# Attention outputs of two four-head units gathered in one PSUM bank, post-processed once per eight heads

## The reference

```python
x = x + 0.5 * ffn(layernorm(x), weight, bias, delta_w, delta_act)
x = x + attn(layernorm(x), wq, bq, wk, bk, wv, bv)
x = x + 0.5 * ffn(layernorm(x), weight, bias, delta_w, delta_act)

# attn: q, k, v = projections; rotary embedding on q and k; per head of 8 features:
scores = einsum('bhqd,bhkd->bhqk', q, k) / sqrt(8)
out = einsum('bhqk,bhkd->bhqd', softmax(scores), v)
```

## Time and profile before

| | us |
|---|---|
| runs | 550.89, 562.03, 566.96 |
| median | 562.03 |
| profiled execution | 559.28 |
| its span from first to last instruction | 557.5 |
| mean granted TensorE clock in it, share of full speed | 0.938 |

### The profile page before, as it was taken

One profiled execution on the slowest core, in us unless ns is written; L12 is line 12 of the kernel. 1 busy time (PEld: TensorE's weight loads), 2 busy tenths in 40 slices (PEclk: granted clock), 3 DMA queues, 4 the chain that ended last, 5 costly groups with the idle time before them and its releaser, 6 DMA issues.

```text
span 557.5 us, 10137 instructions
## 1 busy us (share of the span) xinstructions
PE 473.2 (85%) x2628; PEld 165.2 (30%) x2628; DVE 438.8 (79%) x1020; ACT 389.1 (70%) x754; POOL 229.7 (41%) x350
## 2 busy tenths in 40 slices
PE   2141889999999989999899889999999999998851
PEld 1121232333233333433233223333233323322211
DVE  6646999887998797978897688978897789888025
ACT  5556149787878776688768676878768787777840
POOL 8100156326662555437552564436553534112310
PEclk9985599999999997999899998999899999999995
DMA  6013411221122212221123112221222022200000
GB/s 170 7 47 89 127 51 48 88 86 50 49 87 86 69 50 63 71 88 30 55 84 106 41 48 86 76 68 30 71 79 89 31 76 87 76 3 2 20 1 19
DMA packets 27967, 34.89 MB, mean 63 GB/s; under 512 B 6278, under 2 KB 21260, under 8 KB 27916
## 3 DMA queue, kind: packets, MB, share of 16 engines
q1 hardware_dynamic: 26284, 33.94, 20.1%
q10 hardware_dynamic: 1632, 0.39, 0.3%
HBM read 21.34 MB, written 8.39 MB: 53 GB/s over the span
## 4 chain that ended last, share of the span: by engine, by line
PE 60%; DVE 18%; issue 8%; ACT 7%; POOL 5%; DVEq 1%; DMA 0%; POOLq 0%; ACTq 0%; SPq 0%
PE ot L1120 19%; PE sc L1107 16%; PE st L1096 13%; DVE negmax L893 8%; PE misc L1085 3%; PE misc L1043 3%; ACT probs L645 2%; PE misc L1060 2%; ACT feat_k L535 2%; DVE stats_f L761 1%; DVE amax_f L785 1%; PE misc L1068 1%; PE misc L1038 1%; PE misc L1077 1%; PE misc L1051 1%
## 5 line engine op out<-in xcount | busy, mean ns | idle before, releaser
L893 DVE TENSOR_REDUCE negmax<-sc 128x1 f32<-128x512 f32 x512 | 331.5, 683 | 60.8 <-PE sc L1107 60.0
L645 ACT ACTIVATE probs<-st 128x512 f32<-128x512 f32 x512 | 272.3, 602 | 78.4 <-PE st L1096 75.4
L1107 PE MATMUL sc<-feat_k,feat_q 96*128 96x512 bf16 x512 | 189.4, 398 | 11.8 <-DVE negmax L893 11.1
L1096 PE MATMUL st<-feat_q,feat_k 99*128 99x512 bf16 x512 | 160.3, 386 | 7.8 <-ACT probs L645 6.8
L1120 PE MATMUL ot<-probs,vfeat 128*32 128x512 f32 x1024 | 139.5, 618 | 1.0 <-ACT probs L645 1.0
L1107 PEld LDWEIGHTS sc<-feat_k,feat_q 96*128 96x128 bf16 x512 | 50.1, 98 | 167.8 <-DVE negmax L893 126.2
L1096 PEld LDWEIGHTS st<-feat_q,feat_k 99*128 99x128 bf16 x512 | 49.9, 99 | 80.7 <-ACT probs L645 51.9
L452 POOL TENSOR_SCALAR maxparts<-negmax 128x16 bf16<-128x16 f32 x32 | 8.3, 258 | 70.3 <-DVE negmax L893 70.3
L1027 PE MATMUL misc<-identb,xq_f 128*128 128x128 bf16 x64 | 6.8, 235 | 34.9 <-DVE xq_f L837 34.8
L494 POOL TENSOR_TENSOR xres<-xres,onorm 128x128 f32 (+1 forms) x31 | 14.1, 454 | 53.3 <-DVE onorm L910 53.3
L636 ACT COPY outT<-ot 128x512 f32<-128x512 f32 x32 | 18.8, 586 | 18.7 <-PE ot L1120 18.7
(11 more groups left out here) (134 smaller groups left out, 488.1 us busy)
## 6 DMA issues: line engine op xcount, KB each, us to landing
feat_q<-parts_q SPq DMA_DIRECT2D x96, 96.0 KB
feat_k<-parts_k SPq DMA_DIRECT2D x96, 96.0 KB
qkswap<-qkpre SPq DMA_DIRECT2D x32, 128.0 KB, 2.0
parts_q<-qkparts_q SPq DMA_DIRECT2D x24, 128.0 KB, 2.4
parts_k<-qkparts_k SPq DMA_DIRECT2D x24, 128.0 KB, 2.3
xres<-in_L_attn_x_dram SPq DMA_DIRECT2D x8, 256.0 KB, 4.6
out_dram<-xres SPq DMA_DIRECT2D x8, 256.0 KB, 2.4
feat_q<-maxrows ACTq DMA_DIRECT2D x32, 12.0 KB
```

Source lines behind the costliest of these rows:

```text
L645: nc.scalar.activation(probs[:, s % US, j * S:(j + 1) * S], st[:, bank(2 * s + j), :], ACT.Exp, scale=SCALE).then_inc(exp_done, 1)
L893: nc.vector.tensor_reduce(negmax[:, g, j:j + 1], sc[:, bank(16 * g + j), :], AX.X, ALU.max, negate=True).then_inc(sc_maxed, 1)
L1096: nc.tensor.matmul(st[:, bank(2 * s + j), :], feat["k"][par][0:MROWS, h, kb * P:(kb + 1) * P], feat["q"][par][0:MROWS, h, :], start=True, ...
L1107: nc.tensor.matmul(sc[:, bank(16 * g + j), :], feat["q"][par][0:SROWS, h, t * P:(t + 1) * P], feat["k"][par][0:SROWS, h, :], start=True, s ...
```

## The change

`times_v` of an odd unit now adds to the same bank as that of the even unit before it. For that the values of the heads of odd units are put 16 columns further to the right in their 32 (`values`), with the column of ones beside them; the columns of the other unit of the pair are zero, so each of the eight `times_v` of a pair adds zeros to the rows of the other unit. Only the first call of a pair starts the accumulation. `pairs` keeps only the turns of odd units: copy, transposes, reciprocal, normalisation and residual addition run once per pair, with the shapes of one unit for copy and transposes, 32 instead of 16 elements per row for the reciprocal, two products instead of one for the normalisation, and one addition of 256 elements per row in place of two of 128. The value copy becomes two of half the size, and the fills two more. The post-processings at slots 12 and 28 are gone, those at slots 4 and 20 stay.

```diff
@@ -122,4 +122,4 @@
         outT = sb("outT", [P, S])
-        recip = sb("recip", [P, T, UH])
-        onorm = sb("onorm", [P, T, UH, HD])
+        recip = sb("recip", [P, T, UH, 2])
+        onorm = sb("onorm", [P, T, 2, UH, HD])
         negmax = sb("negmax", [P, G, UH * T])
@@ -241,2 +241,15 @@
 
+        def values(par, u):
+
+            v = vfeat[par].rearrange("p t (g u i) v -> p (t g) u i v", u=2, i=UH)
+            return v[:, :, u, :, VW // 2 * u:VW // 2 * u + HD + 1]
+
+        def pair_of(b, g):
+
+            return 2 * b + g // 2
+
+        def pairs(u):
+
+            return [turn for turn in u if turn[2] % 2 == 1]
+
         def gate(eng):
@@ -378,3 +391,4 @@
                 fill(vfeat[i][:, :, :, :], 0.0)
-                fill(vfeat[i][:, :, :, HD:HD + 1], 1.0)
+                for u in range(2):
+                    fill(values(i, u)[:, :, :, HD:HD + 1], 1.0)
             assert done[0] == FILLS
@@ -489,7 +503,6 @@
 
-                u = G * b + g
-                pool.wait_ge(o_normed, u + 1)
-                n = UH * HD
-                cols = xb(b).rearrange("p (t d) -> p t d", t=T)[:, :, n * g:n * (g + 1)]
-                nc.gpsimd.tensor_tensor(cols, cols, onorm[:, :, :, :].rearrange("p t h d -> p t (h d)"),
+                n = 2 * UH * HD
+                pool.wait_ge(o_normed, pair_of(b, g) + 1)
+                cols = xb(b).rearrange("p (t d) -> p t d", t=T)[:, :, n * (g // 2):n * (g // 2 + 1)]
+                nc.gpsimd.tensor_tensor(cols, cols, onorm[:, :, :, :, :].rearrange("p t u i d -> p t (u i d)"),
                                         ALU.add).then_inc(x_attended, 1)
@@ -500,3 +513,3 @@
                         split_max(nb, g)
-                    for nb, _, g in turns_of_unit(b, par, s, OUT["add"], -1):
+                    for nb, _, g in pairs(turns_of_unit(b, par, s, OUT["add"], -1)):
                         if not hurried("f2", nb) or g < G - 1:
@@ -602,4 +615,5 @@
                     act.wait_ge(pv_done, 16 * (b - 1))
-                nc.scalar.copy(vfeat[par][:, :, :, 0:HD], misc[:, :].rearrange("p (t h d) -> p t h d", t=T, d=HD)
-                               ).then_inc(v_ready, 1)
+                v = misc[:, :].rearrange("p (t u i d) -> p t u i d", u=2, i=UH, d=HD)
+                for u in range(2):
+                    nc.scalar.copy(values(par, u)[:, :, :, 0:HD], v[:, :, u, :, :]).then_inc(v_ready, 1)
 
@@ -633,4 +647,4 @@
                 act.wait_ge(pv_done, 4 * u + 4)
-                if after(u):
-                    act.wait_ge(ot_turned, u)
+                if after(pair_of(b, g)):
+                    act.wait_ge(ot_turned, pair_of(b, g))
                 nc.scalar.copy(outT[:, :], ot[:, :]).then_inc(ot_out, 1)
@@ -656,3 +670,3 @@
                         load_max_rows(nb, npar, g)
-                    for nb, _, g in turns_of_unit(b, par, s, OUT["copy"], -1):
+                    for nb, _, g in pairs(turns_of_unit(b, par, s, OUT["copy"], -1)):
                         copy_out(nb, g)
@@ -755,3 +769,3 @@
                 else:
-                    dve.wait_ge(x_attended, G * b + G)
+                    dve.wait_ge(x_attended, 2 * b + 2)
                 if after(2 * b):
@@ -897,6 +911,5 @@
 
-                u = G * b + g
-                o = misc[:, :].rearrange("p (t h v) -> p t h v", t=T, v=VW)
-                dve.wait_ge(ot_turned, u + 1)
-                nc.vector.reciprocal(recip[:, :, :], o[:, :, :, HD]).then_inc(ot_recip, 1)
+                o = misc[:, :].rearrange("p (t i u v) -> p t i u v", t=T, i=UH, u=2)
+                dve.wait_ge(ot_turned, pair_of(b, g) + 1)
+                nc.vector.reciprocal(recip[:, :, :, :], o[:, :, :, :, HD]).then_inc(ot_recip, 1)
 
@@ -904,10 +917,10 @@
 
-                u = G * b + g
-                o = misc[:, :].rearrange("p (t h v) -> p t h v", t=T, v=VW)
-                dve.wait_ge(ot_recip, u + 1)
-                if after(u):
-                    dve.wait_ge(x_attended, u)
-                nc.vector.tensor_tensor(onorm[:, :, :, :], o[:, :, :, 0:HD],
-                                        recip[:, :, :].unsqueeze(3).broadcast_to([P, T, UH, HD]), ALU.mult
-                                        ).then_inc(o_normed, 1)
+                o = misc[:, :].rearrange("p (t i u v) -> p t i u v", t=T, i=UH, u=2)
+                dve.wait_ge(ot_recip, pair_of(b, g) + 1)
+                if after(pair_of(b, g)):
+                    dve.wait_ge(x_attended, pair_of(b, g))
+                for u in range(2):
+                    ins = nc.vector.tensor_tensor(onorm[:, :, u, :, :], o[:, :, :, u, 0:HD],
+                                                  recip[:, :, :, u].unsqueeze(3).broadcast_to([P, T, UH, HD]), ALU.mult)
+                ins.then_inc(o_normed, 1)
 
@@ -915,7 +928,6 @@
 
-                u = G * b + g
-                dve.wait_ge(o_normed, u + 1)
-                n = UH * HD
-                cols = xb(b).rearrange("p (t d) -> p t d", t=T)[:, :, n * g:n * (g + 1)]
-                nc.vector.tensor_tensor(cols, cols, onorm[:, :, :, :].rearrange("p t h d -> p t (h d)"),
+                n = 2 * UH * HD
+                dve.wait_ge(o_normed, pair_of(b, g) + 1)
+                cols = xb(b).rearrange("p (t d) -> p t d", t=T)[:, :, n * (g // 2):n * (g // 2 + 1)]
+                nc.vector.tensor_tensor(cols, cols, onorm[:, :, :, :, :].rearrange("p t u i d -> p t (u i d)"),
                                         ALU.add).then_inc(x_attended, 1)
@@ -925,3 +937,3 @@
                     mb, _, mg, ms = ahead(b, par, s)
-                    for nb, _, g in turns_of_unit(b, par, s, OUT["turn"] + 1, -1):
+                    for nb, _, g in pairs(turns_of_unit(b, par, s, OUT["turn"] + 1, -1)):
                         invert_sums(nb, g)
@@ -1063,3 +1075,3 @@
 
-                misc_free((v_ready, b + 1))
+                misc_free((v_ready, 2 * b + 2))
                 nc.tensor.matmul(misc[:, :], ones3[:, :], bias3[:, 0:D].unsqueeze(1).broadcast_to([PARTS, T, D]),
@@ -1080,5 +1092,4 @@
             def turn_out(b, g):
-                u = G * b + g
-                pe.wait_ge(ot_out, u + 1)
-                misc_free((o_normed, u + 1))
+                pe.wait_ge(ot_out, pair_of(b, g) + 1)
+                misc_free((o_normed, pair_of(b, g) + 1))
                 for t in range(T):
@@ -1113,6 +1124,6 @@
                 if kb == 0:
-                    if after(u):
-                        pe.wait_ge(ot_out, u)
+                    if g % 2 == 0 and after(pair_of(b, g)):
+                        pe.wait_ge(ot_out, pair_of(b, g))
                     if g == 0:
-                        pe.wait_ge(v_ready, b + 1)
+                        pe.wait_ge(v_ready, 2 * b + 2)
                 pe.wait_ge(exp_done, 2 * (US * u + UH * (kb // 2 + 1)))
@@ -1121,3 +1132,3 @@
                                            probs[:, UH * (kb // 2) + i, S * (kb % 2):S * (kb % 2 + 1)],
-                                           start=kb == 0, stop=kb == T - 1)
+                                           start=(g % 2, kb) == (0, 0), stop=(g % 2, kb) == (1, T - 1))
                 ins.then_inc(pv_done, 1)
@@ -1146,3 +1157,3 @@
                         turn_max(nb, g)
-                    for nb, _, g in turns_of_unit(b, par, s, OUT["turn"], -1):
+                    for nb, _, g in pairs(turns_of_unit(b, par, s, OUT["turn"], -1)):
                         turn_out(nb, g)
@@ -1165,3 +1176,3 @@
 WQ_STEP, VEC_STEPS = 15, 20
-FILLS, BIAS_STEP = 7, 17
+FILLS, BIAS_STEP = 9, 19
 TABLES, ACT_STEPS = 12, 17
```

## The result

| | before | after |
|---|---|---|
| median of 20 runs, us | 562.42 | 560.76 |
| lowest and highest | 550.89, 567.92 | 558.58, 565.70 |
| profiled execution | 559.28 | 561.92 |
| its span | 557.5 | 559.9 |
| mean granted TensorE clock | 0.938 | 0.933 |

The ratio after to before is 1.0078, with a 95% interval of 1.0048 to 1.0109; it compares only the undisturbed runs, which of before are its faster ones (five of its twenty lie within 1.5% of its fastest), and so it points the other way than the medians, whose ratio is 0.997. So within 2% it is the same. That the change makes the kernel slower is not shown by this; the 0.989 that I had forecast lies outside the interval. The profiled span became 2.4 us longer.

The account below looks back on a forecast made before the run. TensorE was taken to bound most of the chain (60%), VectorE slots 7 to 16. Terms 4.4 + 2.5 - 0.5 - 0.45 gave about 6.0 us off 562.0, so 556.0 us (1.1% less), range 547 to 564.

Parts of the forecast that it names:

- slot 28, turns gone: Slot 28: eight transpose turns, on the chain in all eight batches, go; gain 4.4 us.
- slots 12 and 13, turns, reciprocal, product gone: Slots 12 and 13: eight turns with reciprocal and product go; gain 2.5 us, lower bound 0.
- slots 5 to 7, doubled work: Slot 5: VectorE 0.22 us later, idle gap of 0.15 ahead of slot 7; loss 0.5 us, 1.5 without gap.
- slots 3 and 4, two value copies: ScalarE's value copy split in two, 0.16 us more per batch; taken as nothing, 1.3 us if uncovered.
- slots 22 and 23, `misc` held longer: Bank held 0.22 us longer at slot 21, slot 22's turn waits; taken as nothing, upper bound 1.5 us.
- tail: Behind the last unit: second product, longer reciprocal and 256-element addition are uncovered; loss 0.45 us.
- What bounds the kernel: TensorE has 60% of the chain, slot 17 to batch end; slots 7 to 16 lie mostly on VectorE.
- VectorE itself gets rid of 0.36 in slot 13: Slot 13: VectorE sheds reciprocal 0.16 and product 0.20 us, counted in seven batches, all but batch 0: 2.5 us.
- The clock: four stretches of the same length: Slots 9 to 12: four low-clock TensorE stretches stay, a 6.5 us one costing about 3.5; no term in the sum.
- B: Rival: all 10.2 us of TensorE's removed work pays, with one 3.5 us low-clock stretch less; 548.3 us, chance 0.25.
- C: Rival: doubled stage at slots 5 and 21 costs 1.8 + 1.5 us, slot 13 brings nothing; 561.4 us, chance 0.14.
- D: Rival: TensorE pauses in slots 12 to 16, further 3.5 us low-clock stretches in slots 13 to 18; to 580.5, chance 0.06.

Follow-up runs that it names:

- clean pair: b_unroll_poolgate and a_unroll_poolgate: kernels before and after, both with loop written out and an empty GpSimd increment, the change their only difference; 548.38 and 544.15 us.
- b_unroll_poolgate: Kernel before with the loop written out and one empty increment on GpSimd ahead of each lowest-part subtraction of queries and keys; 548.38 us, ratio 0.9866.
- a_unroll_poolgate: Changed kernel with the loop written out and one empty increment on GpSimd ahead of its two subtractions a batch; 544.15 us, ratio 0.9789 to before.
- a_unroll_nmpool: Changed kernel with the loop written out and the two 4-element scalings moved from VectorE to GpSimd; 545.61 us, ratio 0.9879 to before.
- repeated pair: a_rep and b_rep: the changed kernel and the kernel before, both unedited, profiled a second time; 556.38 and 557.9 us (the latter one run).
- a_rep: Changed kernel, no edit, profiled a second time and timed against before; 556.38 us, ratio 1.0031.
- b_rep: Kernel before, no edit, profiled a second time; 557.9 us (one run).
- b_poolgate: Kernel before, loop kept, with one empty increment on GpSimd ahead of each lowest-part subtraction of queries and keys; 551.20 us, ratio 0.9848.

## Why the prediction was wrong, point by point

In the clean pair every slot can be set against its partner. Sums over eight batches, us:

| term | forecast | measured |
|---|---|---|
| slot 28, turns gone | -4.4 | -4.50 |
| slots 12 and 13, turns, reciprocal, product gone | -2.5 | -0.28 (all in batch 0) |
| slots 5 to 7, doubled work | +0.5 | +0.10 |
| slots 3 and 4, two value copies | 0 (up to 1.3) | +0.36 |
| slots 22 and 23, `misc` held longer | 0 (up to 1.5) | +0.33 |
| all other slots | 0 | -0.72 |
| tail | +0.45 | +0.44 |
| sum | -5.95 | -4.3 (-4.2 by the spans) |

- **What bounds the kernel** was read rightly for slot 28, and the term came out within 0.1 us. The tail too.
- **"VectorE itself gets rid of 0.36 in slot 13"** was mis-sized: 2.5 us forecast, 0.28 found, near the lower bound that I had named, and that in batch 0, the one that I had left out. In b_unroll_poolgate, batch 2:

```profile
213.05 0.42 DVE L852 TENSOR_SCALAR magic_f<-p_f 128x512 f32<-128x512 f32 x1
...
213.98 0.25 DVE L897 RECIPROCAL recip<-misc 128x16 f32<-128x16 f32 x1
...
214.69 0.28 DVE L906 TENSOR_TENSOR onorm<-misc,recip 128x128 f32<-128x128 f32 x1
...
214.88 0.68 DVE L781 TENSOR_REDUCE amax_f<-xn_f 128x16 f32<-128x512 f32 x1
214.89 1.28 POOL L432 TENSOR_TENSOR p_f<-xs_f,magic_f 128x512 f32<-128x512 f32 x1
...
216.07 0.17 DVE L785 TENSOR_SCALAR amax_f<-amax_f 128x16 uint32<-128x16 uint32 x1
...
216.25 1.05 POOL L436 TENSOR_TENSOR xq_f<-p_f,amax_f 128x512 bf16<-128x512 f32 x1
...
216.75 0.58 DVE L789 TENSOR_SCALAR amax_f<-amax_f 128x16 f32<-128x16 f32 x1
...
219.41 0.39 PE L1103 MATMUL sc<-feat_k,feat_q 96*128 96x512 bf16 x1 [0.61 <-DVE negmax L889]
```

and a_unroll_poolgate:

```profile
211.63 0.42 DVE L866 TENSOR_SCALAR magic_f<-p_f 128x512 f32<-128x512 f32 x1
...
213.16 0.68 DVE L795 TENSOR_REDUCE amax_f<-xn_f 128x16 f32<-128x512 f32 x1
...
213.47 1.27 POOL L446 TENSOR_TENSOR p_f<-xs_f,magic_f 128x512 f32<-128x512 f32 x1
...
214.35 0.42 DVE L799 TENSOR_SCALAR amax_f<-amax_f 128x16 uint32<-128x16 uint32 x1
...
214.82 1.05 POOL L450 TENSOR_TENSOR xq_f<-p_f,amax_f 128x512 bf16<-128x512 f32 x1
...
215.29 0.61 DVE L803 TENSOR_SCALAR amax_f<-amax_f 128x16 f32<-128x16 f32 x1
...
217.98 0.39 PE L1114 MATMUL sc<-feat_k,feat_q 96*128 96x512 bf16 x1 [0.61 <-DVE negmax L903]
```

From `magic_f` to `amax_f` VectorE gained 0.30 us (1.83 to 1.53). Then its next small step takes 0.42 instead of 0.17 and ends at 214.77, with GpSimd's `p_f` (213.47 + 1.27 = 214.74), which begins 1.84 us behind `magic_f` in both kernels. The step after that ends with GpSimd's `xq_f` in both (215.90 and 215.87; 217.33 and 217.30). So VectorE's small steps wait for GpSimd, whose steps of the quantisation set the pace. From `magic_f` to TensorE's `sc` it is 6.36 and 6.35 us, no gain. The chain of waits showed VectorE there; that VectorE stood behind GpSimd in the same stretch I had only as a bound.
- **Doubled stages and reciprocal:** hidden nearly in full; the reciprocal's 0.10 instead of 0.02 did not matter.
- **"The clock: four stretches of the same length", 3.5 us each.** The level and the rows were right; the cause and the price not. Of the 3.5 us between the earlier trace rows's two batches, 1.0 is the lost race at 205.40 itself: the "2.42 of 4 us busy" of the earlier trace rows holds TensorE's wait for it. A stretch of 3.4 us alone costs 1.5 (slot 16 of a_unroll_nmpool, 5.38 in its one slowed batch, 3.84 in its neighbours).
- **The step that failed** is the sum itself: it counts instructions as time only. With 40 fewer instructions ahead of it, TensorE's loop stood at a place from which its jump is slow: 4.0 us, as much as the change brings. No term and no rival stood for that. The second step that failed is the 2.5 us of slots 12 and 13.
- **How far the pairs add up.** The first profiled pair: -4.2 for the change, +4.0 for the jump, 3 x 0.95 = +2.9 for three more lost races make +2.7; measured +2.4. That is so close by luck, for the clock has no term in it. Batch 1 of after has a stretch of low clock that before has not, batch 2 of before has one of 6.8 us that after has not, and batches 3 and 4 of after have 17.1 us of it against 10.2; these nearly cancel. The repeated pair, with 5 lost races in both, does not add up so: -4.2 and +4.0 make -0.2, and the spans differ by +3.1 (559.2 and 556.1). a_rep has 23.9 us of low clock against 10.2 in b_rep, and only 6.8 of them stand behind the jump. In traces with 5 lost races the changed kernel had 13.7 to 30.7 us of low clock, before 10.2 twice. Whether the change itself makes such stretches longer is not shown.
- **The rivals.** B fell: no batch gained over 1.1 us. C gave nearly the right time, 561.4, for a wrong reason. D's sign (low clock in slots 13 to 18) did not come in after, where the clock was low in slots 10 to 12 and behind the jump; in a_rep one stretch of 10.2 us ran from slot 9 into slot 13. In the versions with the scalings on GpSimd a stretch stood in slot 16, of both kernels alike.
- The range held the median, with help of luck: the change was worth less than forecast and the jump took that back. What the forecast said of the change against before, 1.1% less, was not what happened; a batch at the full clock became 0.52 us shorter (58.05 to 57.53), not 0.9.

## What to carry to other kernels

Look at the jump instruction of each engine and at the count of instruction fetches before crediting an edit in or ahead of a hardware loop: an edit of 40 instructions shifted the loop to a place where the jump is slow, and 24 empty instructions in idle set-up (8 were too few), or writing the loop out, undid it. Look for small VectorE instructions whose duration has two values; one empty instruction on either engine decided this race in all five batches of every trace that had it. And where VectorE's small steps end together with GpSimd's, work taken off VectorE there is given back.

## What the runs showed of the hardware

- TensorE's jump back takes 0.24 or 3.5 to 4.1 us for the same loop, with a second halt of 1.0 to 2.5 us some instructions later; it depends on where the loop stands in the code. The short form has 16 or 17 fetches in the page's part 3, the long one 25 or 27 (the written-out loop, which has no jump, 20 or 21). That the boundary is one of 256 rests on one pair (216 against -40) and the place of the second halt; other offsets than these five (0, 8, 24 in the change, 0 and 216 before) were not tried.
- A 4-element scaling on VectorE took 0.16 or 1.16 us; it was short with GpSimd's start 14 to 21 ns ahead and long with 18 to 28. Where GpSimd began 0.10 us behind or 0.06 ahead it was short or long every time. The same code lost 2 of 5 in one execution and 5 of 5 in another. Why an execution falls on one side was not found.
- The runs of before spread over 17 us (550.9 to 567.9). With the race decided they lay within 3.5 (b_poolgate, 4 runs), written out besides within 0.7 (b_unroll_poolgate, 6 runs).
